# Normalised rows and mean squares: from VectorE to ScalarE

## The reference

```
x = x + tanh(g_xattn) * cross_attention(layernorm(x), context)
x = x + tanh(g_ffn)   * block(layernorm(x))
block(z): z = z + self_attention(rms(z)*w_ln1);  h = rms(z)*w_ln2
          z + routed_experts(h) + shared_expert(h)
layernorm(x) = (x - mean) / sqrt(var + 1e-5);  rms(z) = z / sqrt(mean(z*z) + 1e-6)
```

## Time and profile before

| | |
|---|---|
| median of 3 runs | 933.66 us (932.69 to 934.49) |
| profiled execution | 933.32 us, span 931.5 us, mean granted clock 0.992 |
| PE busy | 903.3 us, 97% |
| PEld busy | 844.4 us, 91% |
| DVE busy | 635.5 us, 68% |
| ACT busy | 558.9 us, 60% |
| POOL busy | 322.6 us, 35% |

### The profile page before, as it was taken

The page is one execution under the profiler, slowest core; times in us unless marked ns, Lnnn a source line. Parts: engine busy times, 40 slices in busy tenths (PEclk is TensorE's granted clock), DMA queues, the critical chain, the costliest instruction groups (busy, mean ns, idle before and its releaser), DMA issues.

```text
span 931.5 us, 16531 instructions
## 1 busy us (share of the span) xinstructions
PE 903.3 (97%) x5915; PEld 844.4 (91%) x5915; DVE 635.5 (68%) x1482; ACT 558.9 (60%) x1448; POOL 322.6 (35%) x344
## 2 busy tenths in 40 slices
PE   7999999999999999999999999899999999999996
PEld 7989999999998999999987877789999999999896
DVE  3557777663446777674287895757595989988864
ACT  3666666663555666664332776755436778778761
POOL 3432323335551222234643542335401232424121
PEclk8999999999999999999999999999999999999999
DMA  5733720006450000001642111114438999999975
GB/s 151 222 94 107 201 83 2 6 18 172 143 160 20 17 1 1 2 12 47 168 115 86 48 52 53 46 60 113 122 95 284 285 343 311 324 314 321 298 199 152
DMA packets 112762, 122.22 MB, mean 131 GB/s; under 512 B 9888, under 2 KB 77928, under 8 KB 112681
## 3 DMA queue, kind: packets, MB, share of 16 engines
q1 hardware_dynamic: 97806, 98.80, 33.9%
q0 software_dynamic: 5184, 12.13, 6.0%
q10 hardware_dynamic: 9690, 10.24, 3.9%
HBM read 110.72 MB, written 19.07 MB: 139 GB/s over the span
## 4 chain that ended last, share of the span: by engine, by line
PE 68%; DVE 14%; DMA 8%; ACT 4%; issue 3%; POOL 1%; SPq 0%; ACTq 0%; DVEq 0%; POOLq 0%
PE bank L2074 61%; PE bank L2222 4%; DVE we L1357 3%; DMA eraw<-in_L_ffn_w_gate_e_dram 2%; DMA eraw<-in_L_ffn_w_down_e_dram 1%; DMA raw<-in_L_xattn_Wq_dram 1%; DVE wf L1357 1%; DMA sums<-s_sum 1%; DMA raw<-s_unit 1%; ACT we L930 1%; PE bank L2415 1%; POOL wx L1926 1%; DVE sm L1583 1%; DMA X<-in_x_dram 1%; DVE stat L1619 1%
## 5 line engine op out<-in xcount | busy, mean ns | idle before, releaser
L1943 POOL TENSOR_SCALAR SC<-SC,mx,anyv 100x361 f32<-100x361 f32 x128 | 81.4, 647 | 211.9 <-DVE mx L1468 200.9
L1357 DVE TENSOR_TENSOR we<-eraw,we 128x704 fp32r<-128x704 f32 (+2 forms) x140 | 107.5, 799 | 22.2 <-ACT we L930 16.7
L930 ACT ACTIVATE we<-eraw 128x704 fp32r<-128x704 f32 (+2 forms) x140 | 96.5, 718 | 35.9 <-DMA eraw<-in_L_ffn_w_gate_e_dram 17.5
L1926 POOL TENSOR_TENSOR wx<-raw,wx 128x512 fp32r<-128x512 f32 x64 | 83.8, 1318 | 72.8 <-ACT wx L916 72.6
L1926 POOL TENSOR_TENSOR wf<-raw,wf 128x512 fp32r<-128x512 f32 x54 | 71.6, 1331 | 106.0 <-ACT wf L916 106.0
L2074 PE MATMUL bank<-H2h,wf 128*128 128x400 f32 x352 | 100.2, 351 | 0.0
L1046 ACT ACTIVATE SC<-SC,mx 100x361 f32<-100x361 f32 x128 | 75.4, 593 | 29.1 <-DVE mx L1464 28.3
L1357 DVE TENSOR_TENSOR Kl<-bank,Kh 128x362 fp32r<-128x362 f32 x64 | 34.1, 534 | 60.3 <-ACT Kh L1004 60.2
L1357 DVE TENSOR_TENSOR QOl<-bank,QOh 128x200 fp32r<-128x200 f32 (+1 forms) x96 | 41.4, 432 | 46.0 <-ACT QOh L959 36.0
L2074 PE MATMUL bank<-XTh,wx 128*128 128x400 f32 x256 | 71.5, 353 | 1.1 <-POOL wx L1926 1.0
L916 ACT ACTIVATE wf<-raw 128x512 fp32r<-128x512 f32 x100 | 61.8, 629 | 17.8 <-DMA raw<-s_unit 8.7
(11 more groups left out here) (291 smaller groups left out, 2733.9 us busy)
## 6 DMA issues: line engine op xcount, KB each, us to landing
raw<-s_unit SPq DMA_DIRECT2D x60, 256.0 KB
eraw<-in_L_ffn_w_gate_e_dram SPq DMA_DIRECT2D x40, 352.0 KB
eraw<-in_L_ffn_w_up_e_dram SPq DMA_DIRECT2D x40, 352.0 KB
eraw<-in_L_ffn_w_down_e_dram SPq DMA_DIRECT2D x40, 256.0 KB
raw<-in_L_xattn_Wq_dram SPq DMA_DIRECT2D x32, 256.0 KB
raw<-in_L_xattn_Wo_dram SPq DMA_DIRECT2D x32, 256.0 KB
eraw<-in_L_ffn_w_down_e_dram SPq DMA_DIRECT2D x20, 192.0 KB
s_unit<-in_L_ffn_w_sh_gate_dram SPq DMA_DIRECT2D x11, 256.0 KB, 3.9
```

What stands on the lines that cost most here:

```text
L930: eng.activation(weights("e", u)[0:rows, 0, 0:n], eraw[u % 6][0:rows, 0:n], ACT.Copy).then_inc(sem("act_e"), 1)
L1357: return eng.tensor_tensor(o, src, f32(hi), ALU.subtract)
L1926: eng.tensor_tensor(w[:, 1, :, :], raw[plan.raw[stream, u] % 4][:, :, :], f32(w[:, 0, :, :]), ALU.subtract).then_inc(sem("pool_w"), 1)
L1943: eng.tensor_scalar(sc, sc, m[:, 3, h:h + 1], anyv[:, b:b + 1], ALU.mult, ALU.mult).then_inc(sem("pool_p"), 1)
```

## The change

ScalarE makes Z = rs * XR + nb with nb = -mean * rs, which VectorE now makes in one 100x1 instruction. ScalarE waits for that nb between its second root instruction and the store of XR. The three earlier waits for Z's memory (the causal constants, the zero rows) move along. In `er`, VectorE keeps only the addition to Z; ScalarE squares Z with a running sum into ms, writing the squares over XR, and the division by 512 becomes the scale of the logarithm. The order of the steps is unchanged; on ScalarE `er` was empty but for one wait.

```
-        def inverse_root(o, var, eps):
+        def inverse_root(o, var, eps, scale=1.0):
-            eng.activation(o, var, ACT.Ln, bias=eps).then_inc(sem("act_own"), 1)
+            eng.activation(o, var, ACT.Ln, bias=eps, scale=scale).then_inc(sem("act_own"), 1)
...
 (ScalarE, norm1)
             act.wait_ge(sem("dve_x1"), b + 1)
+            act.wait_ge(sem("dve_nb"), b + 1)
+            act.wait_ge(sem("pool_const"), CONST["causal"])
+            if b >= HB:
+                act.wait_ge(sem("dma_zero"), 16 * 3)
+            eng.activation(Z[:, b, :], XR[:, b % HB, :], ACT.Identity, bias=mvz[:, b, 1:2], scale=rs[:, b:b + 1]).then_inc(sem("act_z"), 1)
             eng.dma_start(s_sum[b * T:(b + 1) * T, :], XR[:, b % HB, :]).then_inc(sem("dma_st1"), 16)
...
 (ScalarE, new)
+        def er(h, i):
+            b = h * HB + i
+            if b == 0:
+                act.wait_ge(sem("pe_qk"), 16)
+            act.wait_ge(sem("dve_x2"), b + 1)
+            act.wait_ge(sem("dma_st1"), 16 * B)
+            eng.activation(XR[:, i, :], Z[:, b, :], ACT.Square, accum_out=ms[:, b:b + 1]).then_inc(sem("act_ms2"), 1)
 (ScalarE, eroot)
-            act.wait_ge(sem("dve_ms2"), b0 + HB)
-            inverse_root(rz[:, b0:b0 + HB], ms[:, b0:b0 + HB], eps2[:, 0:1]).then_inc(sem("act_rz2"), 1)
+            act.wait_ge(sem("act_ms2"), b0 + HB)
+            inverse_root(rz[:, b0:b0 + HB], ms[:, b0:b0 + HB], eps2[:, 0:1], 1.0 / D).then_inc(sem("act_rz2"), 1)
...
 (VectorE, norm1)
-            if b >= HB:
-                dve.wait_ge(sem("dma_zero"), 16 * 3)
-            eng.tensor_scalar(Z[:, b, :], XR[:, b % HB, :], mv[:, b, 0:1], rs[:, b:b + 1], ALU.subtract,
-                              ALU.mult).then_inc(sem("dve_z"), 1)
+            stt(mvz[:, b, 1:2], mv[:, b, 0:1], -1.0, rs[:, b:b + 1], ALU.mult, ALU.mult).then_inc(sem("dve_nb"), 1)
             stt(ms[:, b:b + 1], mv[:, b, 1:2], rs[:, b:b + 1], rs[:, b:b + 1], ALU.mult, ALU.mult).then_inc(sem("dve_ms1"), 1)
 (VectorE, row)
-            dve.wait_ge(sem("dve_z"), b + 1)
+            dve.wait_ge(sem("act_z"), b + 1)
 (VectorE, er)
             eng.tensor_tensor(Z[:, b, :], banks[plan.bank["er", h, i]][0:T, :], Z[:, b, :], ALU.add).then_inc(sem("dve_x2"), 1)
-            dve.wait_ge(sem("dve_x2"), b + 1)
-            chained(eng.bn_stats(stat[:, b, :], Z[:, b, :]))
-            chained(eng.bn_aggr(mvz[:, b, :], stat[:, b, :]))
-            stt(ms[:, b:b + 1], mvz[:, b, 0:1], mvz[:, b, 0:1], mvz[:, b, 1:2], ALU.mult, ALU.add).then_inc(sem("dve_ms2"), 1)
```

More of the change, by code:

```diff
@@ L1310, in scalar_program @@
                 eroot(*a)
-            elif name == "er" and a == [0, 0]:
-                act.wait_ge(sem("pe_qk"), 16)
+            elif name == "er":
+                er(*a)
             elif name == "eh":
```

## The result

Over six runs each, the changed kernel takes 938.97 us (937.95 to 940.71) and the kernel before 933.82 (932.69 to 934.49): ratio 1.0061 (1.0048 to 1.0074), 5.7 us slower by the ratio (5.2 by the medians). The forecast was 3.5 slower, 937.2. By the ratio the result lies at the upper edge of the stated range of 932.8 to 939.5: 939.4 on the median of before that the forecast started from, 939.52 on the one of six runs. Direction and places were right, the size was too small.

The account below looks back on a forecast made before the run. The prediction took the chain of waits as the bound, TensorE carrying 68% and VectorE 14%. Its terms, 0 - 0.4 + 0.6 + 1.8 + 1.7 = +3.7 us, gave 937.2 us on the medians, range 932.8 to 939.5.

Parts of the forecast that it names:

- D: Mean squares of half 1, 632 to 646 us: squares delay the table load and HR, +1.8 us (1.4 to 2.2).
- that Z ends at 643.6: Half 1's mean squares: the last addition to Z ends at 643.6 instead of 643.1 us.
- second fall of the clock: Half 0's mean squares, behind a 1.8 us hole before 595.6: possible, same price; two falls give +5.4, 939.0.
- C: Mean squares of half 0, 588 to 601 us: squares hold up exponentials, +0.6 us at its end (0.5 to 0.9).
- Prices: Instruction costs: Identity 0.83 us, Square 0.63, reading its sum 0.19, square to next instruction 0.61.
- A: Normalisation of batches 0 to 3, 245 to 264 us: ScalarE's added work and waits are covered, cost 0.
- B: Normalisation of batches 4 to 7, 473 to 512 us: TensorE's wait on PQ shrinks, -0.4 us (0 to -0.68).
- The clock: TensorE's stall before 645.80 us grows to about 2.5, bringing one fall of its clock in half 1, +1.7 us.
- The sum: Whole kernel: 0 - 0.4 + 0.6 + 1.8 + 1.7 = +3.7 us, 937.2 us on the medians.
- that no new fall comes: Rival on TensorE's clock: the hole is split or small products suffice; +2.0, 935.6 us; chance 0.23.
- everything hide: Rival: all hides but batches 4 to 7 and half 0's squares, which cancel; 933.8 us; chance 0.12.
- ScalarE's idle time absorbs the squares: Rival: VectorE's relief decides, the table load stays hidden; -2.2, 931.5 us; chance 0.12.

Follow-up runs that it names:

- rows_only: The kernel before with only the normalised rows moved to ScalarE, the mean squares staying on VectorE; 933.39 us, ratio 1.0004.
- squares_half1: The kernel before with squares on ScalarE in half 1 alone, rows and half 0 as before; 939.14 us, ratio 1.0047.
- squares_half0: The kernel before with squares on ScalarE in half 0 alone, rows and half 1 as before; 934.89 us, ratio 1.0018.
- last_behind_load: The kernel after with one square, that of batch 7, moved behind the table load; 936.10 us, ratio 1.0028.
- warm_gap: The kernel after with twelve unread products on TensorE ahead of its turn of half 1's first row; 937.96 us, ratio 1.0046.
- defer_both: The kernel after with every square issued one step later on ScalarE, half 1's last behind the table load; 933.77 us (0.9987), repeated 932.87 us (0.9991).
- squares_only: The kernel before with only the mean squares moved to ScalarE, the normalised rows staying on VectorE; 939.40 us, ratio 1.0058.

## Why the prediction was right and wrong

**The step that failed** is D's term of +1.8 us: TensorE's added wait for HR measured 2.9 (3.58 against 0.67), outside its bounds of 1.4 to 2.2, because "that Z ends at 643.6" was 1.06 too early. Beside it, the second fall of the clock in C was named but stood at nothing in the sum; C, entered with +0.6, measured 2.98 in this profile. By the stretches the sum is 3.2 us too small: 1.0 of it lies in D and 2.4 in C, where part is the chance named above.

- **Prices**: right. Identity 0.816 (0.83 forecast), Square 0.632 (0.63), the read of the sum 0.186 (0.19), the next instruction 0.63 after a square's start (0.61).
- **A**: right, 0. ScalarE waited 0.31 to 0.34 us for nb before each of the four Identity (the first at 247.01 us), and nothing followed: over 240 to 270 us no kernel's lateness moves by more than 0.01.
- **B**: right. -0.4 forecast, -0.48 to -0.51 in the nine profiles with rows on ScalarE, 0.00 or 0.01 in the four without.
- **C**: mechanism right, size short. I had the scores of the next batch at 595.9; they start at 594.37, which plus the lead of 1.39 at 588 us is 595.76. +0.6 forecast for the whole stage (0.5 to 0.9), 0.93 as a stall. The second fall of the clock, named as possible but left out of the sum, came: a hole of 1.64 where 1.8 was forecast. The fall stands at 595 or 596 in five of the six kernels that run half 0's full squares in front of the exponentials, and in none of the others. In the sum C was 2.98. Part of that is chance: rows_only and squares_half1, whose code in C is that of before, came out at 0.86 and 1.33 with the later fall twice as long as in the profile of before. Set against them the squares cost C 1.7 to 2.1: the stall of 0.93 and about 1 for the new fall. The 1.7 that the ratio of squares_half0 gives agrees.
- **D**: mechanism right, the term "that Z ends at 643.6" too small. Less the 1.59 by which the kernel after is late when D begins, its last Z ends at 645.57 + 0.68 - 1.59 = 644.66: 1.06 later. HDh stood exactly where I had it (639.59 - 1.59 = 638.0). What I had priced at 0.56 was VectorE's next instruction HDl: 1.34 and, one step on, 0.89, together 1.11 too much. ScalarE's weight copy, delayed by the square, had released GpSimd's subtraction into just that moment (639.76 for 1.30). The rest, from the last Z to HR, was forecast as 3.05 and took 3.16. So +1.8 became +2.9. last_behind_load, which keeps both slow HDl (1.34 and 0.90), still has 1.32 in D.
- Two engines side by side, again: HDl reads two SBUF tiles and stretched from 0.56 to 1.34 beside GpSimd's subtraction. In the kernel before, the addition to Z, which reads one bank and one SBUF tile, ran beside such subtractions and stayed at 0.68, and where HDl met one at 641.9 it was GpSimd's that took longer (1.76, alone 1.3):

```profile
636.13 0.68 DVE L1617 TENSOR_TENSOR Z<-bank,Z 100x512 f32<-100x512 f32 x1
636.21 2.54 POOL L1926 TENSOR_TENSOR wf<-raw,wf 128x512 fp32r<-128x512 f32 x2 [2.06 <-ACT wf L916]
...
641.88 1.76 POOL L1926 TENSOR_TENSOR wf<-raw,wf 128x512 fp32r<-128x512 f32 x1 [3.13 <-ACT wf L916]
641.93 0.57 DVE L1357 TENSOR_TENSOR HDl<-TM,HDh 128x400 fp32r<-128x400 f32 x1
```

In the kernel before HDl lasts 0.56 or 0.57 each time, and my 0.56 came from there. The Trainium skill, page "SBUF — State Buffer", section "SBUF: two separate sides", says that of a VectorE instruction with two SBUF inputs and a GpSimd one, whichever starts first holds the shared ports for its whole length and the other waits. By that rule HDl would start when GpSimd ends, 639.76 + 1.30 = 641.06, and end 0.4 to 0.6 later (an estimate from its 0.56); it ended at 641.48. The trace agrees.
- **The clock**: one new fall in D, 1.7 forecast, 1.5 by the stretch and 1.6 by warm_gap: the price was right. That it fell is in part luck: I expected it behind a hole of 2.5. Holes of 3.58 and 3.59 brought it in the three kernels that had one, holes of 2.31, 2.00 and 0.82 did not, and none of 2.5 was run. Had D been as short as forecast, its fall might not have come.
- **The sum**: B -0.5, C +3.0, D +4.5 gives +7.0 in this profile and, with C at 0.93, +4.9 without the second fall. With C at 1.7 to 2.1, against kernels whose later fall is equally long, it gives 5.7 to 6.1; the ratio says +5.7 (4.5 to 6.9). How often C's clock falls one profile of each kernel does not tell.
- **Rivals**: that no new fall comes did not hold; nor did everything hide, as D's hole shows. That ScalarE's idle time absorbs the squares is refuted for this order and true for another: with the squares deferred, D is 0.15 and the total can't be told from the kernel before. Another table did not occur: both kernels have seven table loads, so the squares ran without one of their own.

## What to carry to other kernels

An instruction moved to an idle engine brings its wait along: price not its duration but everything queued behind it, down to a table load that was hidden. Place it where its operand is already there, one step later; here that made the difference between 939 and 933 to 934 us with the same work. When a queue slips, look at who gets released by the slipped instructions and what they then run beside. Where two engines meet, the rows before may show the other one paying, so ask what each would pay. A stage that repeats badly between profiles needs more than one profile before its cost is read.

## What the runs showed of the hardware that I had not expected

- The price of a clock fall depends on what is behind it: 1.5 to 1.6 us where TensorE had solid work (D), but removing the one in C of the kernel before moved that stage by 0.5 us, removing one twice as long from defer_both moved it by 1.4, and neither total moved clear of noise.
- The same hole of 1.63 to 1.64 us in C was followed by a fall in five of six profiles, not in squares_only; a hole of 2.31 in D brought none.
- Beside GpSimd's subtraction a VectorE instruction of 0.56 us with two SBUF inputs lasted 1.34 in the kernel after; in the kernel before the same instruction kept 0.57 and the subtraction went from 1.3 to 1.76. An addition with one input from a bank kept 0.68.
- Runs of one kernel differ by up to 1.1% (930.75 to 941.10 us for the kernel before on one chip), while the stretches B and D of the traces repeat to 0.1 us. Effects under 1 us were read from stretches, not from totals.
